# A mixed attention and expert kernel whose attention orders and PSUM banks are taken from a list planner

## The chip, the cores and the metric

The kernel runs on one core of one Trainium2 chip. The metric is the device time of the whole launch in microseconds (us). The core's engines, as the profile names them, are PE (TensorE, matmuls; PEld is its loading of weights), ACT (ScalarE), DVE (VectorE), POOL (GpSimd) and SP (SyncE, which here only issues DMAs). Each works through its own queue in order, and a step waits on semaphores for steps of other engines.

## What is computed

The reference is a cross-attention with 16 heads of 32 and then a mixture of 8 experts, in which every expert takes its best 512 of the 4096 tokens. Cut to what matters:

```python
x = x + attention(layernorm(x), ctx)     # x, ctx: 8 x 512 x 512
#   q = h @ Wq + bq, k = ctx @ Wk + bk, v = ctx @ Wv + bv
#   softmax(q k^T / sqrt(32)) v, then @ Wo + bo
xf = layernorm(x).reshape(4096, 512)
prob = softmax(xf @ Ws + bs).T           # 8 experts
vals, routes = top_k(prob, 512)
h = gelu(xf[routes] @ W1 + b1)           # 512 x 2048, per expert
out = (h @ W2 + b2) * vals               # added to x at routes
```

## The kernel before

Attention runs in 32 groups: 8 batches of 512 tokens, and in each of them 4 groups of 4 heads (r is the group's number within its batch, 0 to 3). Products with weights keep 32-bit accuracy by splitting each operand in a high and a low part and adding three matmuls, so a projection of a group is 12 matmuls of 512 columns for K and 12 for Q, the values 48 a batch, the output projection 48 a batch.

A group g passes through these steps, named as in the code:

- proj (K and Q, two groups ahead): PE, then the high part on ACT, the low part on DVE (proj_lo); SP writes both to memory (keep_hi, keep_lo) and reads them back in a stacked form (stack_hi, stack_lo) into kst and qst, of which there are three each.
- max (one group ahead), 16 tiles: PE multiplies (L1730), DVE takes each row's extreme (L1339), ACT computes the exponentials in place for the sums (sum, L1143). The tile's bank is returned only then. Then rows: PE transposes the maxima (L1747), ACT and DVE split them (L1134, L1347), and POOL copies them by two small DMAs into qst (rows_lo, L1037). The scores of the group wait for these rows.
- score, 16 tiles: PE (L1762), exponential on ACT into one of six buffers p_ring (L1155); att: for every four of them PE multiplies with the values into the single bank ps_att (L1773). After the fourth att of a group comes divide on DVE (L1371), then osplit and osplit_lo.
- per batch: loading and splitting of the context and of x (csplit, stats, norm, turn), the values v (L1685), the two halves of the output projection (outa, out), the second norm (x1_norm), and the router (route, logits, back).

Seven of the eight PSUM banks (ps_gen) are shared by all steps but att. A class Agenda holds one list of steps. attention_agenda walks through the groups in 20 slots each, with the 16 scores and the 4 att steps at fixed slots, and puts every other step at a hand-set place in units of a group: MAX_AT = ((-0.11, 0.59), ...) by r, ROWS_AT = 0.70, END_MAX_AT for the last group's maxima, and so on. The list in order of these places is the order of TensorE's queue. Each other engine takes the same list, shifted by hand-set lags by kind (order_of). Banks go round: take_bank gives the bank that was given longest ago and is not kept open by a projection:

```python
    def take_bank(self, key):
        i = next(k for k in self.bank_order if k not in self.bank_open)
        self.bank_order.remove(i)
        self.bank_order.append(i)
```

The steps before group 0 (first loads, weights, the first projections and maxima) are listed by hand. After attention come the choice of tokens by bisection, and the experts.

## Time and profile before

| | |
|---|---|
| median of 3 runs | 1729.57 us (1729.15 to 1729.82) |
| span of the profiled execution, first to last instruction | 1729.0 us |
| mean granted TensorE clock, as a share of 2.4 GHz | 0.973 |
| PE, DVE, ACT, POOL busy | 1620.6, 1110.7, 983.9, 303.9 us |
| DMA traffic | 217.27 MB, mean 126 GB/s |

The profiled execution is one run, and its span is 0.6 us below the median of the runs. Starts in the rows are microseconds from the span's start. A row of instructions gives start, duration, engine, line of the kernel, operation, tile written and tiles read, and in square brackets how long the engine had been idle before and what ended the wait. Matmuls overlap: the next one starts before the last one ends, so the distance of the starts is what one costs.

### The profile page before, as it was taken

What the parts mean: (1) busy time and instruction counts of PE and PEld (TensorE: products, weight loads), DVE (VectorE), ACT (ScalarE), POOL (GpSimd) and SP (SyncE); (2) the same over time, 40 slices, a digit from 0 to 9 for tenths busy, and PEclk for the clock granted to TensorE, in tenths of its full rate; (3) what the DMA queues carried; (4) which work ended last, traced back from release to release, by engine and by line L of the source; (5) the groups of instructions that cost most, each with busy time, mean ns of one, the idle gap of its engine ahead of it and who ended that gap; (6) DMA issues with size and microseconds to landing.
All of it is one profiled execution on the core that took longest, in us unless ns stands there. A gap on an engine that the chain in (4) does not pass through costs nothing.

```text
span 1729.0 us, 22299 instructions
## 1 busy us (share of the span) xinstructions
PE 1620.6 (94%) x7847; PEld 1163.4 (67%) x7847; DVE 1110.7 (64%) x1950; ACT 983.9 (57%) x2115; POOL 303.9 (18%) x396
## 2 busy tenths in 40 slices
PE   7889899899898998999987699999999999999997
PEld 5546566566565664655644488788888888888885
DVE  7576876867768678587664566766454545454543
ACT  5798897987988979888875222223232323232321
POOL 5121221311303112113012010102020202020110
PEclk9999899999999999999989899999999999999999
DMA  5452744635436436263351132435243433334340
GB/s 180 122 170 68 214 120 126 176 96 169 138 92 197 141 123 182 65 205 122 111 183 63 43 123 98 120 107 152 98 139 111 114 131 96 136 99 151 97 123 25
DMA packets 131271, 217.27 MB, mean 126 GB/s; under 512 B 17116, under 2 KB 51056, under 8 KB 131160
## 3 DMA queue, kind: packets, MB, share of 16 engines
q1 hardware_dynamic: 114520, 173.23, 32.3%
q0 software_dynamic: 16640, 42.61, 8.9%
q8 instruction: 63, 1.03, 0.3%
q14 instruction: 48, 0.39, 0.1%
HBM read 157.45 MB, written 57.82 MB: 125 GB/s over the span
## 4 chain that ended last, share of the span: by engine, by line
PE 79%; DVE 9%; ACT 6%; issue 3%; DMA 2%; SPq 0%; POOL 0%; DVEq 0%; POOLq 0%
PE ps_gen L751 8%; PE ps_gen L753 8%; PE ps_gen L752 8%; PE ps_gen L1926 7%; PE ps_gen L1928 7%; PE ps_gen L1927 7%; PE ps_att L1773 6%; PE ps_gen L1730 5%; PE ps_gen L1762 5%; PE ps_gen L1712 3%; ACT ps_gen L1143 3%; PE ps_gen L1713 3%; PE ps_gen L1714 3%; ACT p_ring L1155 2%; DVE stat L1243 2%
## 5 line engine op out<-in xcount | busy, mean ns | idle before, releaser
L1339 DVE TENSOR_REDUCE nmax<-ps_gen 128x1 f32<-128x512 f32 x512 | 338.3, 684 | 128.4 <-PE ps_gen L1730 127.7
L1143 ACT ACTIVATE ps_gen<-ps_gen,nmax 128x512 f32<-128x512 f32 x512 | 343.2, 675 | 57.7 <-DVE nmax L1339 57.7
L1155 ACT ACTIVATE p_ring<-ps_gen,keep_scale 128x512 f32<-128x512 f32 x512 | 336.5, 695 | 61.9 <-PE ps_gen L1762 61.9
L1212 ACT ACTIVATE gel<-ps_gen,b_cols 128x512 f32<-128x512 f32 x128 | 88.3, 690 | 448.8 <-PE ps_gen L753 448.7
L1594 DVE TENSOR_TENSOR gel_lo<-gel,gel_hi 128x512 fp32r<-128x512 f32 x126 | 87.2, 692 | 281.6 <-ACT gel_hi L1213 277.3
L1730 PE MATMUL ps_gen<-kst,qst 97*128 97x512 f32 x512 | 208.2, 429 | 16.8 <-ACT ps_gen L1143 11.2
L1762 PE MATMUL ps_gen<-qst,kst 99*128 99x512 f32 x512 | 195.3, 432 | 16.0 <-ACT ps_gen L1143 11.8
L751 PE MATMUL ps_gen<-hT_hi,w_hi 128*128 128x512 f32 x512 | 202.2, 395 | 0.2 <-DVE hT_lo L1587 0.2
L753 PE MATMUL ps_gen<-hT_hi,w_lo 128*128 128x512 f32 x512 | 199.5, 390 | 0.0
L752 PE MATMUL ps_gen<-hT_lo,w_hi 128*128 128x512 f32 x512 | 199.4, 389 | 0.0
L1926 PE MATMUL ps_gen<-w_hi,gel_hi 128*128 128x512 f32 x504 | 198.1, 393 | 0.0
L1928 PE MATMUL ps_gen<-w_hi,gel_lo 128*128 128x512 f32 x504 | 196.5, 390 | 0.0
L1927 PE MATMUL ps_gen<-w_lo,gel_hi 128*128 128x512 f32 x504 | 196.3, 389 | 0.0
L1773 PE MATMUL ps_att<-p_ring,v_sb 128*32 128x512 f32 x1024 | 147.5, 650 | 4.1 <-ACT p_ring L1155 4.0
L1762 PEld LDWEIGHTS ps_gen<-qst,kst 99*128 99x128 f32 x512 | 95.3, 197 | 79.9 <-issue 30.4
L1730 PEld LDWEIGHTS ps_gen<-kst,qst 97*128 97x128 f32 x512 | 98.4, 195 | 63.1 <-ACT ps_gen L1143 24.2
L1065 POOL DMA_INDIRECT out_x<-y_out,idx x28 | 49.5, 1768 | 511.1 <-ACT y_out L1232 504.7
L1143 ACT ACTIVATION_READ_ACCUMULATOR ps_gen<-ps_gen,nmax 128x1 f32 x512 | 113.4, 221 | 0.0
L753 PEld LDWEIGHTS ps_gen<-hT_hi,w_lo 128*128 128x128 f32 x512 | 96.1, 188 | 20.6
L751 PEld LDWEIGHTS ps_gen<-hT_hi,w_hi 128*128 128x128 f32 x512 | 96.2, 188 | 19.5 <-issue 0.6
L752 PEld LDWEIGHTS ps_gen<-hT_lo,w_hi 128*128 128x128 f32 x512 | 96.2, 188 | 19.3
L1928 PEld LDWEIGHTS ps_gen<-w_hi,gel_lo 128*128 128x128 f32 x504 | 94.6, 188 | 19.9
(218 smaller groups left out, 2687.4 us busy)
## 6 DMA issues: line engine op xcount, KB each, us to landing
w_raw<-in_L_ffn_W SPq DMA_DIRECT2D x128, 512.0 KB, 3.5
kst<-qk_rows SPq DMA_DIRECT2D x93, 256.0 KB, 3.9
qst<-qk_rows SPq DMA_DIRECT2D x93, 256.0 KB, 5.1
x_in<-in_x POOLq DMA_DIRECT2D x60, 256.0 KB, 3.4
out_x<-x_in SPq DMA_DIRECT2D x32, 256.0 KB, 2.6
qk_rows<-kT_hi SPq DMA_DIRECT2D x31, 256.0 KB, 2.0
qk_rows<-kT_lo SPq DMA_DIRECT2D x31, 256.0 KB, 2.0
qk_rows<-qT_hi SPq DMA_DIRECT2D x31, 256.0 KB, 2.0
```

Of the source, the lines that this page charges most:

```text
L751: e.matmul(psum, lhsT=wh, rhs=mh, start=(i == 0), stop=False)
L752: e.matmul(psum, lhsT=wh, rhs=ml, start=False, stop=False)
L753: last = e.matmul(psum, lhsT=wl, rhs=mh, start=False, stop=(i == n - 1))
L1143: e.activation(psum[:, :], psum[:, :], ACT.Exp, bias=nmax[g % 2][:, c], scale=-1.0, accum_out=den[g % 2][:, c]).then_inc(drained_sem("max" ...
L1155: e.activation(p_ring[n % NP_][:, :], ps("score", g, kt, h)[:, :], ACT.Exp, scale=keep_scale[:, b:b + 1]).then_inc(drained_sem("score", g, ...
L1339: e.tensor_reduce(nmax[g % 2][:, h * TB + t:h * TB + t + 1], ps("max", g, h, t)[:, :], AX.X, ALU.min).then_inc(s_min, 1)
L1730: e.matmul(ps("max", g, h, t)[:, :], lhsT=qst[k][0:ROWS_MAX, h, t * P:(t + 1) * P], rhs=kst[k][0:ROWS_MAX, h, :], start=True, stop=True).t ...
L1762: e.matmul(ps("score", g, kt, h)[:, :], lhsT=kst[k][0:ROWS_ALL, h, kt * P:(kt + 1) * P], rhs=qst[k][0:ROWS_ALL, h, :], start=True, stop=Tr ...
L1773: last = e.matmul(ps_att[h * DH:(h + 1) * DH, :], lhsT=v_sb[:, kt, (c4 * HG + h) * DH:(c4 * HG + h + 1) * DH], rhs=p_ring[((g * KT + kt) * ...
L1926: e.matmul(ps_y[tt], lhsT=gh, rhs=wh, start=(j == 0), stop=False)
L1927: e.matmul(ps_y[tt], lhsT=gh, rhs=wl, start=False, stop=False)
L1928: return e.matmul(ps_y[tt], lhsT=gl, rhs=wh, start=False, stop=(j == NF - 1))
```

## The change

The single list goes. Every step becomes a Part on an engine, with the parts that it comes after, a wanted time, the bank that it takes or gives back, and two costs from a table (how long the engine is occupied, and when the result is seen). Parts of one kind on one engine form a line and keep their order among themselves. Plan.run then goes forward in modelled time: of the parts at the heads of the lines it takes those that can start within LOOK of the earliest, and of these the one with the smallest wanted time. That gives every engine its own order. A part that takes a bank gets the one that is expected back first; HELD limits max tiles to three banks and scores to two. The wanted times are again places in units of a group (K_AT, Q_AT, MAX_AT, SPAN) plus LAG by engine and kind. The steps before group 0 keep their order. The closing steps of a batch's router become steps of their own (choice_max, choice_exp, choice), the special places of the last group's maxima go, and the hand-written end of attention is planned too. The instructions themselves and what each waits for stay as they are. The K projection of the group two after an r=3 group is wanted at -0.698 to -0.096 of it instead of 0.05 to 0.10.

```diff
+class Part:
+
+    def __init__(self, engine, step, at, cost, after, line, takes, frees):
+        self.engine, self.step, self.at = engine, step, at
+        self.busy, self.seen = cost
+        self.after, self.line = after, line
+        self.takes, self.frees = takes, frees
+        self.ready = None
...
+    def add(self, engine, step, at, after=(), line=None, takes=None, frees=None):
+        line = (engine, line or step[0])
+        part = Part(engine, step, at + LAG.get(line, 0), COST[engine][step[0]], after, line, takes, frees)
+        self.parts[(engine,) + step] = part
+        self.lines.setdefault(line, []).append(part)
+
+    def run(self):
+        a = self.agenda
+        for line in self.lines.values():
+            line.sort(key=lambda part: part.at)
+        head = {line: 0 for line in self.lines}
+        lines_of = {engine: [line for line in self.lines if line[0] == engine] for engine in a.order}
+        free = {engine: 0.0 for engine in a.order}
+        bank_free = {i: 1e-3 * n for n, i in enumerate(a.bank_order)}
+        held = {}
+        returned = {kind: [] for kind in HELD}
+        taken = {kind: 0 for kind in HELD}
+
+        def startable(part):
+            start = 0.0
+            for need in part.after:
+                before = self.parts.get(need)
+                if before is None:
+                    continue
+                if before.ready is None:
+                    return None
+                start = max(start, before.ready)
+            if part.takes:
+                if not bank_free:
+                    return None
+                start = max(start, min(bank_free.values()) + 0.05)
+                kind = part.takes[0]
+                if kind in HELD:
+                    n = taken[kind] - HELD[kind]
+                    if n >= len(returned[kind]):
+                        return None
+                    if n >= 0:
+                        start = max(start, sorted(returned[kind])[n])
+            if part.engine == "pe" and start > 0:
+                start += 0.107
+            return max(start, free[part.engine])
+
+        left = len(self.parts)
+        while left:
+            best = None
+            for engine in a.order:
+                able = []
+                for line in lines_of[engine]:
+                    if head[line] < len(self.lines[line]):
+                        part = self.lines[line][head[line]]
+                        start = startable(part)
+                        if start is not None:
+                            able.append((start, part))
+                if able:
+                    first = min(start for start, _ in able)
+                    start, part = min((p for p in able if p[0] <= first + LOOK), key=lambda p: (p[1].at, p[0]))
+                    if best is None or start < best[0]:
+                        best = (start, part)
+            start, part = best
+            left -= 1
+            head[part.line] += 1
+            free[part.engine] = start + part.busy
+            part.start, part.ready = start, start + part.seen
+            a.order[part.engine].append(part.step)
+            if part.takes:
+                i = min(bank_free, key=bank_free.get)
+                del bank_free[i]
+                held[part.takes] = i
+                a.give_bank(part.takes, i)
+                if part.takes[0] in HELD:
+                    taken[part.takes[0]] += 1
+            if part.frees:
+                bank_free[held[part.frees]] = part.ready
+                if part.frees[0] in HELD:
+                    returned[part.frees[0]].append(part.ready)
...
-
-    GAPS = 5 * KT
-    K_AT = ((0.01, 0.35), (-0.13, 0.22), (0.05, 0.15), (0.05, 0.10))
-    Q_AT = ((0.40, 0.42), (0.21, 0.30), (0.14, 0.34), (0.17, 0.32))
-    MAX_AT = ((-0.11, 0.59), (-0.07, 0.66), (-0.05, 0.67), (-0.17, 0.60))
-    ROWS_AT = 0.70
-    RECIP_AT, RDEN_AT, OSPLIT_AT = 0.03, 0.56, 0.18
-    V_NEXT_AT = (0.32, 1.32)
-    LOAD_C_AT, SPLIT_C_AT = (-0.26, 0.33), (0.29, 0.48)
-    LOAD_X_AT, STATS_X_AT = (0.28, 0.41), (0.66, 0.95)
-    NORM_X_AT, TURN_X_AT = (0.71, 1.05), (0.93, 1.16)
-    HALF_AT, HALF_FOR = (("residual", 0.03), ("add_bias", 0.35), ("outa", 0.49)), 0.76
-    LATE_AT = (("out", 0.20), ("x1_norm", 0.44), ("route", 0.56), ("logits", 0.66), ("back", 0.73))
-    LATE_FOR = 0.74
...
-    END_MAX_AT, END_ROWS_AT = (-0.39, 0.56), 0.68
...
+ENGINES = ("pe", "act", "dve", "pool", "sync")
+COST = {
+    "pe": {"proj": (0.693, 0.89), "max": (0.231, 0.43), "rows": (0.109, 0.31), "rden": (0.436, 0.63), "score": (0.231, 0.43),
+           "att": (1.105, 1.15), "v": (2.74, 2.94), "turn": (0.436, 0.63), "outa": (1.386, 1.59), "osum": (0.693, 0.89),
+           "out": (1.386, 1.59), "route": (0.436, 0.63), "logits": (0.405, 0.52), "back": (0.109, 0.31)},
+    "act": {"proj": (0.585, 0.73), "sum": (0.662, 0.82), "rows": (0.174, 0.30), "score": (0.570, 0.72), "osplit": (0.613, 0.79),
+            "csplit": (0.520, 0.66), "turn": (0.477, 0.64), "logits": (0.157, 0.31), "route": (0.477, 0.64),
+            "choice_exp": (0.136, 0.26), "wsplit": (0.585, 0.72)},
+    "dve": {"proj_lo": (0.658, 0.78), "max": (0.600, 0.72), "rows_lo": (0.313, 0.32), "recip": (0.160, 0.30), "rden": (0.597, 0.72),
+            "divide": (0.592, 0.72), "osplit_lo": (0.659, 0.78), "v": (0.570, 0.72), "csplit_lo": (0.600, 0.72),
+            "stats": (1.020, 1.10), "norm": (0.453, 0.57), "turn_lo": (0.598, 0.72), "outa": (0.600, 0.72), "out": (1.750, 1.80),
+            "x1_norm": (0.453, 0.57), "route": (0.602, 0.72), "back": (0.300, 0.35), "choice_max": (0.330, 0.41),
+            "choice": (0.540, 0.60), "wsplit": (0.660, 0.78), "tables": (0.500, 0.60)},
+    "pool": {"rows_lo": (1.050, 2.60), "recip": (0.560, 0.66), "load": (0.550, 4.00), "load_wo": (0.550, 3.30),
+             "residual": (0.550, 4.00), "stats": (0.600, 0.75), "add_bias": (1.240, 1.39), "out": (0.600, 0.75),
+             "tables": (12.0, 12.0)},
+    "sync": {"keep_hi": (0.360, 2.30), "keep_lo": (0.360, 2.30), "stack_hi": (0.800, 6.00), "stack_lo": (0.400, 5.50),
+             "mask_row": (0.400, 2.50), "out": (0.360, 3.00), "x1_norm": (0.360, 3.00), "choice_out": (0.360, 2.50),
+             "piece_in": (0.800, 3.00)},
+}
+LOOK = 0.023
+HELD = {"max": 3, "score": 2}
+LAG = {
+    ("act", "proj"): 0.065, ("dve", "proj_lo"): 0.032, ("pool", "rows_lo"): -0.605, ("act", "rows"): -0.136, ("dve", "rows_lo"): -0.141,
+    ("sync", "stack_hi"): -0.046, ("sync", "stack_lo"): 0.395, ("pool", "recip"): 0.043, ("dve", "rden"): -0.186, ("dve", "outa"): -0.4,
+    ("dve", "csplit_lo"): -0.274, ("dve", "turn_lo"): 0.082, ("dve", "v"): 0.188, ("dve", "out"): 0.019, ("act", "turn"): 0.006,
+    ("dve", "back"): -0.047, ("act", "osplit"): -0.275, ("dve", "divide"): 0.345, ("act", "logits"): -0.091, ("pool", "add_bias"): -0.545,
+    ("act", "csplit"): -0.079, ("pe", "rows"): 0.166, ("dve", "route"): -0.071, ("dve", "max"): -0.081, ("dve", "recip"): -0.034,
+    ("act", "score"): 0.027, ("act", "sum"): 0.034, ("pe", "score"): -0.219, ("dve", "osplit_lo"): 0.15,
+}
+K_AT = ((0.24, 0.248), (-0.055, 0.281), (0.094, 0.256), (-0.698, -0.096))
+Q_AT = ((0.472, 0.472), (0.34, 0.351), (0.109, 0.318), (0.248, 0.412))
+MAX_AT = ((0.124, 0.67), (0.036, 0.694), (-0.083, 0.753), (0.309, 0.742))
+ROWS_AT, RECIP_AT, RDEN_AT, OSPLIT_AT, ATT_AT = 0.132, 0.197, 0.833, -0.55, 0.042
+SPAN = {
+    "v": (-1, 0.295, 1.594), "load_c": (-3, -0.536, 0.13), "csplit": (-3, -0.167, -0.092), "load_x": (-3, 0.752, 0.887),
+    "stats": (-3, 0.587, 0.597), "norm": (-3, 0.577, 0.856), "turn": (-3, 0.676, 0.826), "residual": (2, -0.159, 0.515),
+    "add_bias": (2, 1.445, 2.219), "outa": (2, 0.138, 0.992), "out": (4, 0.006, 0.738), "x1_norm": (4, 0.603, 1.647),
+    "route": (4, 0.389, 1.208), "logits": (4, 0.608, 1.2), "back": (4, 0.751, 1.343),
+}
+
+
+def spread(span, k, n):
+    return span[0] + (span[1] - span[0]) * (k + 0.5) / n
...
+                p.add("pe", ("max", g, h, t), at, stacks if n == 0 else [], takes=("max", g, h, t))
+                p.add("dve", ("max", g, h, t), at, [("pe", "max", g, h, t), ("pe", "rows", g - 2), ("act", "sum", g - 2, HG - 1, TB - 1)])
+                p.add("act", ("sum", g, h, t), at, [("dve", "max", g, h, t), ("dve", "recip", g - 2)], frees=("max", g, h, t))
...
+            for h in range(HG):
+                n = (g * KT + kt) * HG + h
+                at = g + (kt + h / HG) / KT
+                p.add("pe", ("score", g, kt, h), at, [("pool", "rows_lo", g)], takes=("score", g, kt, h))
+                p.add("act", ("score", g, kt, h), at,
+                      [("pe", "score", g, kt, h), ("pe", "att", *divmod((n - NP_) // HG, KT))], frees=("score", g, kt, h))
+            p.add("pe", ("att", g, kt), g + (kt + 1) / KT + ATT_AT,
+                  [("act", "score", g, kt, HG - 1), ("dve", "v", b, kt), ("dve", "divide", g - 1)])
+        p.add("dve", ("divide", g), g + 1, [("pe", "att", g, KT - 1), ("dve", "rden", g)])
+        used = [("pe", "outa" if r < GB // 2 else "out", b - 1, TB - 1)]
...
-            for kind, *at in steps:
+            for kind, *at in agenda.order["pe"]:
```

## Rows read from the trace of the kernel before

**Rows 1.** The page: span, busy time by engine, chain that ended last, one group of instructions.

```profile
span 1729.0 us, 22299 instructions
...
PE 1620.6 (94%) x7847; PEld 1163.4 (67%) x7847; DVE 1110.7 (64%) x1950; ACT 983.9 (57%) x2115; POOL 303.9 (18%) x396
...
PE 79%; DVE 9%; ACT 6%; issue 3%; DMA 2%; SPq 0%; POOL 0%; DVEq 0%; POOLq 0%
...
L1155 ACT ACTIVATE p_ring<-ps_gen,keep_scale 128x512 f32<-128x512 f32 x512 | 336.5, 695 | 61.9 <-PE ps_gen L1762 61.9
```

**Rows 2.** Stretches: start:end, length, busy us of PE PEld DVE ACT POOL, PEclk, DMA share, GB/s.

```profile
534.00:646.00 112.00, 104.37 (x534) 66.62 (x532) 82.78 (x161) 94.51 (x221) 22.94 (x35) 0.98 0.48 142
...
992.00:1729.00 737.00, 724.52 (x3393) 595.05 (x3391) 407.04 (x571) 200.52 (x318) 89.14 (x64) 0.99 0.37 113
...
81.00:937.00 856.00, 796.89 (x3980) 500.61 (x3980) 615.68 (x1178) 719.47 (x1660) 174.88 (x277) 0.96 0.46 138
```

**Rows 3.** Stretches of one batch, cut where divide (L1371) starts; columns as in rows 2.

```profile
533.50:560.50 27.00, 22.59 (x121) 12.43 (x120) 23.86 (x55) 24.10 (x57) 7.42 (x13) 0.94 0.61 168
560.50:587.10 26.60, 24.42 (x121) 15.24 (x120) 19.65 (x34) 25.52 (x62) 7.56 (x11) 1.00 0.46 139
587.10:615.00 27.90, 27.90 (x137) 19.15 (x136) 15.66 (x27) 22.29 (x51) 2.50 (x4) 1.00 0.35 95
615.00:646.40 31.40, 30.36 (x164) 20.46 (x163) 24.51 (x51) 23.36 (x54) 5.83 (x10) 1.00 0.51 160
```

**Rows 4.** Groups of PE instructions, 81 to 937 us: count, busy us, mean ns, idle before.

```profile
L1730 PE MATMUL ps_gen<-kst,qst 97*128 97x512 f32 x477 | 195.8, 429 | 14.9 <-ACT ps_gen L1143 11.0 <-issue 3.7
L1762 PE MATMUL ps_gen<-qst,kst 99*128 99x512 f32 x494 | 188.0, 431 | 15.4 <-ACT ps_gen L1143 11.3 <-DVE qT_lo L1324 1.8 <-DMA qst<-by_row 1.8
...
L751 PE MATMUL ps_gen<-wv_hi,cT_hi 128*128 128x512 f32 x112 | 43.9, 392 | 0.0
```

**Rows 5.** Timeline of PE, 498 to 513 us.

```profile
499.93 1.06 PE L1773 MATMUL ps_att<-p_ring,v_sb 128*32 128x512 f32 x8
...
505.88 0.39 PE L752 MATMUL ps_gen<-wv_lo,cT_hi 128*128 128x512 f32 x1
506.11 0.39 PE L753 MATMUL ps_gen<-wv_hi,cT_lo 128*128 128x512 f32 x1
```

**Rows 6.** Waits of PE, 81 to 937 us: us in total, times, longest us.

```profile
PE ps_gen L1747 <- DVE nmax L1339: 15.7, 14, 1.4
PE ps_gen L1762 <- ACT ps_gen L1143: 11.3, 17, 1.0
PE ps_gen L1730 <- ACT ps_gen L1143: 11.0, 10, 1.3
```

**Rows 7.** Chain that ended last, 450 to 570 us: start, us, engine, tile, line.

```profile
461.63 0.44 PE ps_gen L1754 x4
...
523.40 0.71 DVE stat L1243
...
525.37 0.53 POOL qst L1037
525.90 3.99 DMA qst<-by_row
```

**Rows 8.** Timeline of PE, 515 to 566 us.

```profile
546.80 0.91 PE L1730 MATMUL ps_gen<-kst,qst 97*128 97x512 f32 x2 [1.21 <-ACT ps_gen L1143]
547.65 1.94 PE L1773 MATMUL ps_att<-p_ring,v_sb 128*32 128x512 f32 x8
```

**Rows 9.** Timelines of PE and SP around 887 us.

```profile
889.12 0.40 PE L1730 MATMUL ps_gen<-kst,qst 97*128 97x512 f32 x1
893.19 0.77 PE L1730 MATMUL ps_gen<-kst,qst 97*128 97x512 f32 x1 [3.67 <-issue]
...
887.11 0.30 SPq L853 DMA_DIRECT2D qst<-qk_rows  x1
```

**Rows 10.** DMA issues, 81 to 937 us: count, KB each, median us to landing.

```profile
qst<-by_row POOLq DMA_DIRECT2D x60, 8.0 KB, 1.7
```

More of the change, by code:

```diff
@@ L67, in __init__ @@
         self.steps = []
-        self.times = []
-        self.now = -3.0
+        self.order = {}
         self.bank = {}
@@ L87, in add @@
     def add(self, *step):
-        if self.now < 0 or self.now >= NG:
-            self.now += 1e-4
         self.steps.append(step)
-        self.times.append(self.now)
-    def order_of(self, lags):
-        def at(n):
-            inside = 0 <= self.times[n] < NG
-            return self.times[n] + (lags.get(self.steps[n][0], 0) if inside else 0)
-        return [self.steps[n] for n in sorted(range(len(self.steps)), key=at)]
     def flush(self):
@@ L324, in attention_agenda @@
-    END_MAX_AT, END_ROWS_AT = (-0.39, 0.56), 0.68
-    places = []
-    def place(start, span, calls):
-        lo, hi = start + span[0], start + span[1]
-        for k, call in enumerate(calls):
-            places.append((lo + (hi - lo) * (k + 0.5) / len(calls), call))
-    def late(kind, b, t):
-        if kind == "residual":
-            a.residual(b, t)
-        elif kind == "out":
-            a.out(b, t)
-        elif kind in ("outa", "route", "logits", "back"):
-            a.with_bank(kind, b, t)
-        else:
-            a.add(kind, b, t)
@@ L371, in attention_agenda @@
-    place(NG - 2, (0.0, 0.1), [(a.add, "piece_in", n) for n in range(3)])
-    place(NG - 2, (0.1, 0.2), [(a.add, "tables")])
-    place(0, (0.0, 0.3), [(a.load_wo, c) for c in range(DC)])
-    place(0, (0.4, 0.85), [(a.add, "wsplit", "o", c) for c in range(DC)])
-    places.sort(key=lambda p: p[0])
-    def fill(time):
-        a.now = time - 1 / GAPS
-        a.flush()
-        while places and places[0][0] < time:
-            call, *args = places.pop(0)[1]
-            call(*args)
-    def attend(g, kt):
-        a.add("att", g, kt)
-        if kt == KT - 1:
-            a.add("divide", g)
@@ L389, in attention_agenda @@
-    for i in range(NG):
-        for kt in range(KT):
-            before = (i, kt - 1) if kt else (i - 1, KT - 1)
-            time = [i + (5 * kt + n) / GAPS for n in range(1, 6)]
-            a.now = i + kt / KT
-            a.with_bank("score", i, kt, 0)
-            a.with_bank("score", i, kt, 1)
-            fill(time[0])
-            if before[0] >= 0:
-                attend(*before)
-            fill(time[1])
-            a.with_bank("score", i, kt, 2)
-            fill(time[2])
-            a.with_bank("score", i, kt, 3)
-            fill(time[3])
-            fill(time[4])
-        a.flush()
@@ L406, in attention_agenda @@
-    a.now = NG + 1.0
-    attend(NG - 1, KT - 1)
-    for t in range(TB):
-        a.osum(B - 1, t)
-    a.osplit(NG - 1)
-    a.flush()
-    for t in range(TB):
-        a.out(B - 1, t)
-        if t > 0:
-            a.add("x1_norm", B - 1, t - 1)
-    a.add("x1_norm", B - 1, TB - 1)
-    for t in range(TB):
-        a.with_bank("route", B - 1, t)
-    for kind in ("logits", "back"):
-        for t in range(TB):
-            a.with_bank(kind, B - 1, t)
+    a.order = {engine: list(a.steps) for engine in ENGINES}
@@ L774, in load_b2 @@
                 e.dma_start(b2_b[k][:, :], b2[ex:ex + 1, :].to_broadcast([P, D])).then_inc(s_b2[k], 16)
[L776 removed]
+            for kind, *at in agenda.order["sync"]:
                 if kind == "first":
@@ L919, in gpsimd_program @@
             e.memset(half[:, :], -0.5).then_inc(s_const, 1)
-            for kind, *at in agenda.order_of(agenda.lags["pool"]):
+            for kind, *at in agenda.order["pool"]:
                 if kind == "picks":
@@ L1083, in scalar_program @@
             on = Waiter(e)
-            for kind, *at in agenda.order_of(agenda.lags["act"]):
+            for kind, *at in agenda.order["act"]:
                 if kind == "turn":
```

274 lines of the change are left out of this document (174 added, 100 removed).

## The prediction, made before the changed kernel was run

> **What bounds the kernel now.** I read the page first. TensorE is busy 94% of the 1729.0 us span, and the chain that ended last is 79% TensorE, 9% VectorE, 6% ScalarE [rows 1]. That mean hides two halves, so I cut the span with the view by stretches [rows 2]. From 992 us on, in the experts, TensorE is busy 724.5 of 737.0 us at clock 0.99; the change does not touch that code. Attention, 81 to 937 us, is another case: 796.9 of 856 us, granted clock 0.96, ScalarE 719.5, VectorE 615.7. "Busy" flatters TensorE here, since a matmul's 0.39 us overlaps the next one's start, 0.23 us later [rows 5].
>
> So I counted the work of a batch (four groups). By the code it has 64 max, 64 score, 96 projection, 48 value and 48 output matmuls of 512 columns. The trace's counts agree: 477 max and 494 score matmuls in the 31 groups of the stretch, 112 for each third of the value product of 7 batches [rows 4]. 320 x 0.23 = 73.6 us. The 16 attention-value steps (eight matmul records each, x8) take 1.06 us each at full clock [rows 5], 17.0 us; at half clock one takes 1.94 us [rows 8]. Twelve groups of four transposes at 0.44 us [rows 7] are 5.3, and logits, single transposes and the like I estimate at 2. Sum: 98 us of TensorE at full clock, against 112 to 114 us that a batch takes. About 14 us a batch, 12%, are lost.
>
> Where? I cut one batch at the starts of the VectorE divide that ends each group (the one from 533.5 to 646.4 us) [rows 3]. First stretch (early r=1): 27.0 us, TensorE 22.6, ScalarE 24.1, VectorE 23.9, clock 0.94. Second (r=2): 26.6 us, ScalarE 25.5. Third (r=3): 27.9 us, TensorE all of it, ScalarE only 22.3. Fourth (r=0 of the next batch): 31.4 us, TensorE 30.4, ScalarE 23.4. So the limits alternate: the exponentials limit two groups, matmuls (values, output projection) the other two, and only the difference between the columns is a stall.
>
> The view of waits names TensorE's own stalls in attention: 15.7 us in 14 pieces where the transpose of the maxima stood at the head of TensorE's queue for the last reduction, 11.3 and 11.0 us where a score or a max matmul waited for ScalarE to give its bank back [rows 6]. Two single places stand out in the timeline. A burst of output tiles on VectorE (the statistics at 523.40) makes the max rows late, and their DMA, issued 525.37, is 3.99 us of the chain [rows 7]. At 889.1 to 893.2 us TensorE stands for a max matmul of the last group, whose operand left SyncE only at 887.11; after it the same matmul shows 0.77 us, half clock [rows 9].
>
> **The change, part by part.** *Instructions.* None is added or removed in attention: same matmuls, exponentials, reductions and DMAs with the same waits. The step that closed a batch's router is split in two, so that VectorE can do something between subtracting the maximum and summing, 0.3 us at most, seven times: 2 us on VectorE, which is not the limit. I take nothing. The experts do not change: 0.
>
> *Banks.* Before, a bank was chosen by rotation in TensorE's order, whichever was free. Now it is the one the plan expects back first, with at most 3 held by max tiles and 2 by scores, leaving 2 for projections and the rest. That aims at the 11.3 + 11.0 us of bank waits. Floor nothing, ceiling 22.3. A score holds a bank for a matmul (0.43 us at L1762's mean [rows 4]) plus an exponential (0.695 [rows 1]): about 1.2 us with the signals between, two banks give one score each 0.6 us, near ScalarE's own pace, so I take the limit of 2 to cost nothing while sums run between scores.
>
> *Order on TensorE.* The transpose of the maxima is no longer placed at a fixed 0.70 of the group; it is queued when the plan sees the last reduction done. That aims at the 15.7 us [rows 6]. But where ScalarE is the limit, removed TensorE idling is only partly time.
>
> *Order on ScalarE and VectorE.* Hand lags become a choice of the earliest startable step. This is what can close the gaps in the first and second stretches. If they ran at ScalarE's busy time, and the other two at TensorE's, a batch would take 24.1 + 25.5 + 27.9 + 30.4 = 107.9 us instead of 112.9: 5.0 us. That is the most that ordering alone gives; more needs matmuls moved from the long stretches into the short ones. The tables do some of that: the K projection wanted in group r=3 goes 0.7 of a group earlier (4 x 3 x 0.23 = 2.8 us), turns and output halves about 0.3 earlier. But these land in r=2, where TensorE already has 24.4 of 26.6 us, so I count no gain for it. The whole batch cannot go under the 98 us of matmul.
>
> I take half of the 5.0 us, 2.5 a batch, over 7 batches: 17.5 us. Half, because ScalarE's busy column overlaps the reading of its accumulator with the next exponential and so overstates what it must do, while each chain matmul, reduction, exponential has latencies that no order removes. The ends are 0 and 35 (7 x 5.0).
>
> *The last groups.* The hand-set place of the last group's maxima, -0.39 of a group, is what put them in front of the queue before their DMA was there [rows 9]. The plan gives these loads 5.5 to 6.0 us and schedules other work first. TensorE idled 3.67 us there and then ran cold; but scores would have waited on the same maxima later. I take 3 of it (0 to 6). After 937 us the output tiles are a VectorE chain that a new order of transposes shortens by 1 us at most; I take 0.
>
> *What the plan gets wrong.* It fixes each queue for durations that never vary. The max rows cost 2.6 us from issue in it. The trace has 0.5 us for issuing and a median of 1.7 to landing [rows 10] for each of two, which agrees, but also 0.53 + 3.99 = 4.5 us in a busy stretch [rows 7], 1.9 more. Scores are pulled 0.219 of a group ahead, so a late row finds TensorE's head blocked. In one boundary of five of the 31: 6 x 0.4 to 1.9 us, I take 3 (0 to 59).
>
> Sum against the profiled 1729.0: - 17.5 - 3 + 3 = -17.5 us, 1711.5. The runs' median of 1729.57 is 0.6 above the span, so 1712; I say **1711**.
>
> The clock. TensorE's granted clock drops to 1.2 GHz about once a batch: two max matmuls at 546.80 after 1.21 us of idling, and then an x8 step taking 1.94 us instead of 1.06 [rows 8]. Fewer pauses should leave fewer of these; at one drop a batch it is worth 1 to 2 us a batch and is inside my 2.5.
> The Trainium skill (TensorE: Matmul & The Clock Gate, section "A second HAM failure mode: psum-queue depth-cycling") speaks against a planner like this one: frequent short pauses between groups of matmuls while cycling through banks can make the clock oscillate. The trace agrees so far only at one place a batch.
>
> **The rivals.**
> *A. The stretches are already at their limits.* For: TensorE is busy 27.9 of 27.9 us in one stretch and 30.4 of 31.4 in another, ScalarE 25.5 of 26.6 in a third [rows 3]; only the first has room. Then I gain 1 us a batch or less and the waits only change names: 1729.6 - 5 = 1724, from 1720 to 1732.
> *B. The plan levels the batch.* TensorE and ScalarE are limits in different groups, and the order now lets ready matmuls fill any gap. If a batch came to 106, that is 7 us each, 49, and 5 at the ends: 1676, from 1665 to 1692. Against: value tiles can't leave PSUM before the batch's last attention steps have read the old ones, and 2 banks remain for them.
> *C. Late rows block the queue (slower).* The mechanism is that of the last part: TensorE reaches the next group's first score when the plan expects the rows, and max matmuls, projections and attention-value steps stand behind it. The gain of 20.5 is used up, and 3.5 more lost, at 24 / 31 = 0.8 us a boundary. With 1.2 us in each, 1729.6 - 20.5 + 37 = 1746. Against: the median landing of 1.7 us fits the plan [rows 10].
> *D. The pauses get shorter and more, and the clock oscillates.* If a further 10 us of each batch ran at 1.2 GHz, with TensorE the limit, that is 5 us x 7 = 35: 1712 + 35 = 1747. The rule cited above is this one. For: one drop a batch already follows a pause of 1.2 us. Against: the clock is 1.00 in three stretches of four [rows 3], though they have many pauses below 1 us.
>
> **How the numbers follow.** My forecast, 1696 to 1720, 0.42; B 0.20; A 0.20; C 0.13; D 0.05. A measurement of this kernel tells about 0.2%, 3.5 us, from no change. Faster: 0.42 + 0.20 + half of A, 0.10, is 0.72. Same: the rest of A, 0.09. Slower: C, D and a trace of A, 0.19. The range leaves out the lower half of B (0.08) and the upper halves of C and D (0.10): 1678 to 1743. Both signs in it; the forecast's own range is 1696 to 1720.
>
> **What would show it.** Right: the divides stand 110 to 111 us apart over a batch instead of 113; TensorE's wait for nmax at the transpose of maxima under 5 us in all (15.7 before); the two bank waits halved; no 3.7 us stop near 890. The first stretch of a batch shrinks most, the third stays at 27.9. Wrong, C: TensorE's score matmuls wait for DMA qst<-by_row for tens of us. Wrong, B: ScalarE over 24.5 us in the stretch that has 22.3 now. Wrong, D: granted clock under 0.93 over attention. Wrong in another way: the busy engine of a stretch is not its limit, the loop through three engines and seven banks is; then the gain would not stand in the first stretch but in all four.

## The result, and the profile after

The changed kernel takes 1691.61 us (median of 4 runs, 1688.73 to 1693.09) against 1729.69 us: 38.1 us less, a ratio of 0.9774 with a 95% interval of 0.976 to 0.9788. The forecast was 1711, with a range of 1678 to 1743. The sign and the range hold; the gain is twice the 18 us that I had worked out. The profiled execution is the one of 1688.73 us, the fastest of the four, with a span of 1686.9; so the two spans differ by 42.1 us, the medians by 38.1.

The page of the changed kernel, the same lines as in [rows 1]:

```profile
span 1686.9 us, 22363 instructions
...
PE 1601.5 (95%) x7847; PEld 1164.9 (69%) x7847; DVE 1113.7 (66%) x1950; ACT 978.3 (58%) x2115; POOL 301.6 (18%) x396
...
PE 82%; DVE 7%; DMA 4%; ACT 4%; issue 2%; POOL 0%; SPq 0%; DVEq 0%; POOLq 0%; ACTq 0%
```

The number of matmuls is the same (x7847). In the chain TensorE has gained three points, ScalarE and VectorE have lost two each, and DMA has doubled, from 2% to 4%. Attention as a whole, which answers to the last line of [rows 2], and a batch cut at the starts of divide, which answers to [rows 3]:

```profile
77.00:893.80 816.80, 779.60 (x3987) 501.71 (x3985) 619.41 (x1178) 715.57 (x1663) 170.56 (x274) 0.98 0.48 144
```

```profile
501.10:531.40 30.30, 29.15 (x158) 18.75 (x159) 28.79 (x63) 29.19 (x69) 11.57 (x19) 1.00 0.65 196
531.40:553.90 22.50, 22.50 (x112) 14.68 (x113) 15.85 (x27) 21.46 (x53) 4.60 (x6) 1.00 0.50 139
553.90:578.70 24.80, 24.80 (x122) 16.53 (x123) 15.74 (x27) 22.48 (x54) 1.16 (x3) 1.00 0.26 74
578.70:605.60 26.90, 26.86 (x156) 17.87 (x156) 23.63 (x49) 21.29 (x50) 5.68 (x10) 1.00 0.61 191
```

Read this beside [rows 3]. The batch takes 104.5 us in place of 112.9. Three of its four stretches are now TensorE from end to end, and the clock is 1.00 in all. TensorE idles 1.2 us in the whole batch; before it was 7.6. The first stretch, the only one in which I had seen room, became longer, 30.3 us for 27.0, and took in 158 TensorE instructions in place of 121. Every other stretch is shorter by 3 to 4.5 us. Work has moved into the first stretch. What moved, the view by stretches says when asked for one line alone: the first of the three matmuls of each K or Q projection step, here the kernel before (its line L1712),

```profile
533.50:560.50 27.00, 2.71 (x7) 1.13 (x6) 0.94 0.61 168
560.50:587.10 26.60, 3.57 (x8) 1.50 (x8) 1.00 0.46 139
587.10:615.00 27.90, 3.42 (x9) 1.50 (x8) 1.00 0.35 95
615.00:646.40 31.40, 3.84 (x10) 1.89 (x10) 1.00 0.51 160
```

and here the changed kernel (L1853):

```profile
501.10:531.40 30.30, 6.08 (x15) 2.83 (x15) 1.00 0.65 196
531.40:553.90 22.50, 2.87 (x7) 1.32 (x7) 1.00 0.50 139
553.90:578.70 24.80, 2.05 (x5) 0.94 (x5) 1.00 0.26 74
578.70:605.60 26.90, 2.07 (x5) 0.94 (x5) 1.00 0.61 191
```

7, 8, 9, 10 have become 15, 7, 5, 5. (A batch has 32 such steps; the rows of before add up to 34, because a matmul that runs across a cut is counted on both sides. The weight loads, the second count, give 6, 8, 8, 10.) Eight more steps of three matmuls at 0.23 us are 5.5 us of TensorE, moved into the stretch where it idled. By the kind of matmul it is the next batch's K projections that moved, from 3 to 11 steps in that stretch; Q stays at 4. The other 13 of the 37 added instructions are three max and three score matmuls and seven transposes of x. In the plan's own list for TensorE, the K projections of the next batch's first two groups come after 1.56 and 1.81 groups' worth of scores; before they came after 2.12 and 3.12 (counted from the start of the batch under way).

The waits of TensorE in attention, which answer to [rows 6]:

```profile
PE ps_gen L1903 <- DMA qst<-by_row: 9.5, 7, 2.9
PE ps_gen L1871 <- DMA qst<-qk_rows: 7.8, 1, 7.8
PE ps_gen L1871 <- DVE qT_lo L1459: 5.5, 6, 0.9
...
PE ps_gen L1871 <- ACT ps_gen L1278: 3.0, 11, 0.8
...
PE ps_gen L1888 <- DVE nmax L1474: 0.8, 1, 0.8
```

The wait of the maxima's transpose is down from 15.7 us to 0.8, the two waits for ScalarE to give a bank back from 22.3 to 3.2. By the code a max matmul that waits for qT_lo waits for a bank too, one that a projection held; that is 5.5 us now. The scores' wait for late rows (L1903) is up to 9.5 us from 1.8. One wait is new: a single 7.8 us.

Where did the 42.1 us between the two spans go? By the starts of divide: to the first one +1.9 (80.9, 82.7); from there over 28 groups to the divide at 873.3 before, 821.3 after, -53.9; over the last three groups, 63.6 before and 72.5 after, +8.9; behind the last divide +1.0. So the full batches gain 7.7 us each, and the end gives 9 back. The 28 groups as one stretch, before and after:

```profile
80.90:873.30 792.40, 742.90 (x3732) 473.47 (x3733) 582.78 (x1116) 667.36 (x1544) 161.71 (x248) 0.97 0.47 140
```

```profile
82.70:821.30 738.60, 718.35 (x3707) 469.58 (x3707) 580.29 (x1106) 656.98 (x1533) 160.06 (x249) 0.99 0.50 149
```

The 53.9 us have three parts. TensorE idles 20.2 us in place of 49.5: 29.3 us. It has 25 matmuls fewer here, since about that many more now run before the first divide (279 for 253): at 0.23 us about 6 us. The rest is mostly the clock: cut into pieces of 2 us, the granted clock adds up to 44 us at 1.2 GHz before and 10 us after. At that level matmuls of 512 columns start 0.43 us apart (those at 409.92 to 411.20, for instance) in place of 0.23, so 34 us less of it are worth up to 16. These three make 51 of the 53.9 us; the clock's part is up to 30% of them.

What happened at the end, the queue of SyncE shows, in the changed kernel from 829 us:

```profile
832.69 0.40 SPq L900 DMA_DIRECT2D w_raw<-in_L_ffn_W  x1
833.13 0.50 SPq L902 DMA_DIRECT2D w_raw<-in_L_ffn_W  x1
...
834.72 1.39 SPq L946 DMA_DIRECT2D qk_rows<-qT_hi  x1
836.14 0.49 SPq L900 DMA_DIRECT2D w_raw<-in_L_ffn_W  x1
836.67 0.86 SPq L902 DMA_DIRECT2D w_raw<-in_L_ffn_W  x1
837.63 0.48 SPq L953 DMA_DIRECT2D qk_rows<-qT_lo  x1
838.15 0.53 SPq L900 DMA_DIRECT2D w_raw<-in_L_ffn_W  x1
838.72 1.55 SPq L902 DMA_DIRECT2D w_raw<-in_L_ffn_W  x1
842.97 0.81 SPq L977 DMA_DIRECT2D qst<-qk_rows  x2
```

and the chain that ended last, and TensorE:

```profile
834.72 8.24 DMA qk_rows<-qT_hi
843.35 8.50 DMA qst<-qk_rows
```

```profile
852.74 1.62 PE L1871 MATMUL ps_gen<-kst,qst 97*128 97x512 f32 x3 [7.77 <-DMA qst<-qk_rows]
```

Of six weight loads of 512 KB, two go out just before the write of the last group's Q and four between that write and the read back: the plan sees SyncE's queue free and knows no bandwidth. The write takes 8.24 us, the stacked read 8.50, and TensorE stands for 7.77.

### The profile page after: what moved, and what is told of

The parts are those of the page before. It is cut to its first block, busy times and chain, and to the rows that moved or that the text cites. A ratio compares the mean times of both kernels' runs of the same rounds, so it can differ in the third digit from the quotient of the medians.

```text
span 1686.9 us, 22363 instructions
## 1 busy us (share of the span) xinstructions
PE 1601.5 (95%) x7847; PEld 1164.9 (69%) x7847; DVE 1113.7 (66%) x1950; ACT 978.3 (58%) x2115; POOL 301.6 (18%) x396
## 4 chain that ended last, share of the span: by engine, by line
PE 82%; DVE 7%; DMA 4%; ACT 4%; issue 2%; POOL 0%; SPq 0%; DVEq 0%; POOLq 0%; ACTq 0%
PE ps_gen L886 9%; PE ps_gen L887 8%; PE ps_gen L888 8%; PE ps_gen L2067 7%; PE ps_gen L2069 7%; PE ps_gen L2068 7%; PE ps_gen L1903 7%; PE ps_gen L1871 6%; PE ps_att L1914 6%; PE ps_gen L1853 3%; PE ps_gen L1854 3%; PE ps_gen L1855 3%; ACT ps_gen L1278 2%; PE ps_gen L1930 2%; PE ps_gen L1931 2%
## 5 line engine op out<-in xcount | busy, mean ns | idle before, releaser
L1474 DVE TENSOR_REDUCE nmax<-ps_gen 128x1 f32<-128x512 f32 x512 | 330.0, 683 | 78.6 <-PE ps_gen L1871 76.7
L1903 PE MATMUL ps_gen<-qst,kst 99*128 99x512 f32 x512 | 196.8, 425 | 10.7 <-DMA qst<-by_row 9.5
L1871 PE MATMUL ps_gen<-kst,qst 97*128 97x512 f32 x512 | 186.6, 423 | 17.9 <-DMA qst<-qk_rows 7.8
L1903 PEld LDWEIGHTS ps_gen<-qst,kst 99*128 99x128 f32 x512 | 95.3, 190 | 96.6 <-issue 66.0
L1871 PEld LDWEIGHTS ps_gen<-kst,qst 97*128 97x128 f32 x512 | 93.8, 191 | 79.8 <-issue 40.1
L1914 PE MATMUL ps_att<-p_ring,v_sb 128*32 128x512 f32 x1024 | 139.5, 617 | 5.4 <-ACT p_ring L1290 5.2
L1200 POOL DMA_INDIRECT out_x<-y_out,idx x28 | 49.5, 1770 | 511.1 <-ACT y_out L1367 504.7
```

The costliest lines, as they stand in the source:

```text
L1474: e.tensor_reduce(nmax[g % 2][:, h * TB + t:h * TB + t + 1], ps("max", g, h, t)[:, :], AX.X, ALU.min).then_inc(s_min, 1)
L1871: e.matmul(ps("max", g, h, t)[:, :], lhsT=qst[k][0:ROWS_MAX, h, t * P:(t + 1) * P], rhs=kst[k][0:ROWS_MAX, h, :], start=True, stop=True).t ...
L1903: e.matmul(ps("score", g, kt, h)[:, :], lhsT=kst[k][0:ROWS_ALL, h, kt * P:(kt + 1) * P], rhs=qst[k][0:ROWS_ALL, h, :], start=True, stop=Tr ...
L1914: last = e.matmul(ps_att[h * DH:(h + 1) * DH, :], lhsT=v_sb[:, kt, (c4 * HG + h) * DH:(c4 * HG + h + 1) * DH], rhs=p_ring[((g * KT + kt) * ...
```

## The experiments

Times are medians with the ratio to the kernel before, run beside them on the same chip (its medians were 1728.52 to 1730.34 us), and the ratio's 95% interval.

**Banks alone.** The kernel before, all orders kept; its lists are run through the plan as one line for each engine.

```diff
+    for engine, kept in head.items():
+        lags = old.lags.get(engine, {})
+        steps = old.steps if engine == "pe" else old.order_of(lags)
...
+                    part.line, part.at = (engine, "all"), at
...
-HELD = {"max": 3, "score": 2}
+HELD = {}
```

> The kernel before with all five engines' orders unchanged, step by step; only the PSUM banks are given out as the plan gives them (the one expected back first), without limits on the banks held. Theory O (the gain of 38 us comes from the orders, which keep TensorE filled in three of four stretches): little, -5 to +3 us against before. Theory K (banks: the waits of 11.3 + 11.0 us for a bank were the price of the rotation): -10 to -20 us, and both waits below 5 us.

1727.72 us, 0.999 (0.9979 to 1.0). Nothing that can be told from no change, as Theory O expected. The waits of max and score matmuls (L2254, L2286) for an exponential of the maxima (L1661) to return a bank fell from 22.3 to 5.8 us, each of the two below the 5 us that Theory K named, but the time did not follow. Waits for an exponential of the scores (L1673), which return banks as well, came in their place, and the transpose's wait for the last reduction rose to 18.1:

```profile
PE ps_gen L2271 <- DVE nmax L1857: 18.1, 14, 1.6
...
PE ps_gen L2286 <- ACT p_ring L1673: 4.2, 7, 0.6
PE ps_gen L2254 <- ACT ps_gen L1661: 4.1, 14, 0.7
...
PE ps_gen L2254 <- ACT p_ring L1673: 2.3, 7, 0.8
PE ps_gen L2286 <- ACT ps_gen L1661: 1.7, 10, 0.2
```

So the waits for ScalarE to return a bank fell by 10 us, from 22.3 to 12.3, and were worth under 2 us of time: where TensorE had waited for a bank, it now waits a little later for something else.

**Orders alone.** The planned orders, step by step, but a turn among the banks:

```diff
+    for part in p.done:
+        if part.takes:
+            i = next(k for k in turn if k in back)
...
+        if part.frees:
+            back.add(holder[part.frees])
```

> The changed kernel with the planned orders unchanged; each step that takes a bank takes the one that was taken longest ago among those whose return stands before it in the plan, in place of the one expected back first. Theory O: 1690 to 1698 us, nearly all of the gain kept. Theory K: 1705 us or more, with TensorE's waits on ScalarE for banks back above 15 us in all.

1748.93 us, 1.0109 (1.0086 to 1.0132): 57 us behind the changed kernel, with the same orders. Theory O falls in this form. The time is Theory K's, its sign is not: TensorE's waits on ScalarE for a bank stay under 7 us in all. TensorE now waits where it did not before, for banks that projections and values hold:

```profile
PE ps_gen L1887 <- DVE qT_lo L1475: 15.9, 20, 1.6
PE ps_gen L1887 <- DVE v_sb L1529: 8.9, 20, 0.5
...
PE ps_gen L1887 <- DVE kT_lo L1475: 5.4, 6, 0.9
```

The turn is counted by the plan's sequence of steps, so a bank can be taken that comes back later than another; the turn of the kernel before itself was not run, since by the lists steps would then wait for each other in a circle. What the run says is that these orders need the banks they were made with.

**Planner with the places of before.** New Plan.run and limits, old wanted times and lags.

```diff
-K_AT = ((0.24, 0.248), (-0.055, 0.281), (0.094, 0.256), (-0.698, -0.096))
+K_AT = ((0.01, 0.35), (-0.13, 0.22), (0.05, 0.15), (0.05, 0.10))
...
-    "v": (-1, 0.295, 1.594), "load_c": (-3, -0.536, 0.13), "csplit": (-3, -0.167, -0.092), "load_x": (-3, 0.752, 0.887),
+    "v": (-1, 0.32, 1.32), "load_c": (-3, -0.26, 0.33), "csplit": (-3, 0.29, 0.48), "load_x": (-3, 0.28, 0.41),
```

> The changed kernel's planner and its limits on the banks, but with the wanted times and the lags by kind that the kernel before has. Theory O1 (the procedure, ready steps first on each engine, makes the gain): 1690 to 1703 us. Theory O2 (the wanted times do, the planner is only their carrier): 1710 to 1735 us, with stretches again at 27, 27, 28 and 31 us.

1766.79 us, 1.0203 (1.0168 to 1.0237). The planner as a procedure is 37 us slower than the hand-set lists if it is fed with their numbers, and slower than either theory allowed. TensorE stands 18.5 us for the second norm (its output, transposed for the router) and 19.9 us, up to 4.2 us at a time, for a max matmul.

**No lags.** `LAG = {}`.

> The changed kernel without the table of lags by engine and kind (all zero); wanted times by group as changed. Theory O1: within 8 us of the changed kernel's 1691.6. Theory O2: 1705 us or more, since the score lag of -0.219 and the late divide and stacks are what orders the engines.

1689.87 us, 0.9774 (0.9757 to 0.979). All 29 lags together are worth nothing that shows. It serves as the base of the next runs, since it is simpler.

**The places in two halves,** both on top of no lags.

```diff
-MAX_AT = ((0.124, 0.67), (0.036, 0.694), (-0.083, 0.753), (0.309, 0.742))
-ROWS_AT, RECIP_AT, RDEN_AT, OSPLIT_AT, ATT_AT = 0.132, 0.197, 0.833, -0.55, 0.042
+MAX_AT = ((-0.11, 0.59), (-0.07, 0.66), (-0.05, 0.67), (-0.17, 0.60))
+ROWS_AT, RECIP_AT, RDEN_AT, OSPLIT_AT, ATT_AT = 0.70, 0.03, 0.56, 0.18, 0.05
```

(and K_AT and Q_AT) for the first; the whole of SPAN for the second.

> The changed kernel without lags, and with the places of before for the steps of a group (K, Q, maxima, rows, reciprocal, denominators, output split); the steps of a batch keep the changed places. Theory G (the group's places carry the gain, by what they let TensorE do early): 1720 us or more. Theory S (the batch's places carry it): below 1705 us.

1705.14 us, 0.9854 (0.9828 to 0.988): 15 us more than its base, a hair outside what Theory S named. So much hangs on the group's places.

> The changed kernel without lags, and with the places of before for the steps of a batch (loads, splits, statistics, turns, values, output halves, router); the group's places as changed. Theory G: below 1705 us. Theory S: 1720 us or more, since TensorE then stands for norms at the turns.

1757.57 us, 1.0148 (1.0111 to 1.0186): 68 us, more than the whole gain, hang on the batch's places: Theory S by the time. Not by its reason, since TensorE does not stand for norms; its longest wait is 15.0 us in all in front of a max matmul.

**No limits on the banks held.** `HELD = {}` in the changed kernel.

> The changed kernel without the limits of 3 banks for max tiles and 2 for scores. If the limits carry the gain: 1710 us or more, because maxima, wanted early, fill the banks and projections find none. If they are only a bound that the order hardly meets: within 5 us of 1691.6.

1799.0 us, 1.0395 (1.0366 to 1.0424), 107 us behind. And with the limit of 3 for max tiles kept, `HELD = {"max": 3}`:

> The changed kernel with only the limit of 3 banks for max tiles, scores unlimited. If the 107 us of e7 are maxima that hold banks for two engines' work: within 8 us of 1691.6. If they are scores run ahead of the exponentials: 1750 us or more.

1759.08 us, 1.0153 (1.0127 to 1.018). So the limit of two for scores is worth 67 us, that for maxima another 40 once the scores have none. Without the score limit the wait of score matmuls for the maxima's rows is the longest, in both runs; here in the run with the limit for maxima alone:

```profile
PE ps_gen L1903 <- DMA qst<-by_row: 31.5, 18, 3.0
```

That is 22 us more than in the changed kernel, a third of the 67. That scores run ahead of the exponentials, as the expectation has it, fits the time; no run shows it apart.

**The pieces of the experts after the last stacked loads.**

```diff
+    landed = [("sync", "stack_" + k, w, NG - 1) for k in ("hi", "lo") for w in "kq"]
     for n in range(3):
-        p.add("sync", ("piece_in", n), NG - 2, done)
+        p.add("sync", ("piece_in", n), NG - 2, landed)
```

> The changed kernel, but the loads of the first three expert pieces come after the four stacked loads of the last group in the plan, in place of between them. If the 3 MB of weights are what makes those loads take 8.2 and 8.5 us in the chain (and the stretch from 821 to 856 us 35 us long): 1680 to 1686 us. If the stretch is long for another reason: 1691 us and no change.

1682.59 us, 0.9731 (0.9702 to 0.976), 9.0 us less than the changed kernel and inside what was expected. The weights go out behind the stacked loads:

```profile
843.29 0.79 SPq L978 DMA_DIRECT2D qst<-qk_rows  x2
...
844.60 0.50 SPq L989 DMA_DIRECT2D qst<-qk_rows  x1
845.20 0.40 SPq L901 DMA_DIRECT2D w_raw<-in_L_ffn_W  x1
```

The last three groups take 62.5 us here, 72.5 in the changed kernel and 63.6 before, and the 7.8 us stop is gone. The same write of Q takes 4.7 us in place of 8.24, and the stacked reads a median of 3.5 in place of 8.50. So the 9 us that the end had given back are these 512 KB loads. (The profiled spans differ by 5.5 us only. In this execution the 28 groups took 3.3 us more, at nearly the same idle time of TensorE, with 24 us at the lower clock in place of 10.)

**Preparing the next batch, and the output side,** each with the places of before, on top of no lags. First loads, split, statistics, norms and turns, then all the rest of SPAN.

> The changed kernel without lags (e4, 1689.9 us), with the places of before for the steps that prepare the next batch alone: loads, split of the context, statistics, norms, turns. Theory P (the 67 us of e6 come from preparing late: projections of the next batch stand for the turned x and the split context): 1725 us or more. Theory Q (they come from the output side): within 8 us of e4.

1757.13 us, 1.0134 (1.0103 to 1.0166): all of e6's loss, so Theory P by the time. TensorE's longest waits are those in front of a max matmul (14.7 us), for exponentials (14.3) and for late rows (13.4), not the projections' own.

> The same, with the places of before for values, residual, bias, output halves, second norm and router alone. Theory P: within 8 us of e4. Theory Q: 1725 us or more.

1714.0 us, 0.9887 (0.9861 to 0.9913): 24 us, between the two expectations. The halves do not add up, 67 and 24 are more than 68; both theories named something.

Then the preparation was split: the context, and x.

```diff
-    "v": (-1, 0.295, 1.594), "load_c": (-3, -0.536, 0.13), "csplit": (-3, -0.167, -0.092), "load_x": (-3, 0.752, 0.887),
+    "v": (-1, 0.295, 1.594), "load_c": (-3, -0.26, 0.33), "csplit": (-3, 0.29, 0.48), "load_x": (-3, 0.752, 0.887),
```

is the first of the two; the second takes load_x, stats, norm and turn back instead.

> The changed kernel without lags (1689.9 us), with the places of before for the loads and the split of the context alone. If the K projections of the next batch, which need the split context, are what must come early: 1715 us or more, and the projection count in the first stretch near 7 again in place of 15. If the turns must: within 8 us of 1689.9.

1735.25 us, 1.003 (1.0013 to 1.0046), 45 us behind its base. The longest stretch of a batch (32.9 us) has 10 projection steps, neither the 15 of the changed kernel nor the 7 of before.

> The same with the places of before for the loads of x, statistics, norms and turns alone. If the context carries it: within 8 us of 1689.9. If the turns must come early: 1715 us or more.

1727.85 us, 0.9996 (0.9975 to 1.0016), 38 us behind. Here the long stretch has 14 projection steps, as good as the changed kernel, and yet takes 33.7 us where that one takes 30.3. The chain in it shows why:

```profile
535.29 5.53 DMA qk_rows<-kT_hi
541.77 3.99 DMA qk_rows<-qT_hi
546.13 3.85 DMA qst<-qk_rows
549.98 2.13 issue
```

A projection that comes late goes to memory and back before its max matmuls can run, and TensorE stood 3.67 us for the first of them. (The profile names no releaser for the last 2.13 us; the read of the low part, issued only at 547.26, may be it.) Such stops add up to 24.5 us in seven places. So preparing early does two things: it gives TensorE matmuls for the stretch where it had none, and it covers the round trip through memory.

**Late rows in the plan.** On top of e8, the plan is told what a busy stretch had shown: `"rows_lo": (1.050, 4.50)` in place of 2.60.

> The kernel of e8 (1682.6 us), with the plan's duration for the maxima's rows raised from 2.60 to 4.50 us, what a busy stretch showed. If late rows at the head of TensorE's queue cost what the waits name (9.6 us): 1675 to 1681 us. If what is put ahead of them instead is no better: 1680 to 1690 us.

1702.32 us, 0.9822 (0.9795 to 0.985), 20 us slower than e8, outside both expectations. The wait for the rows left the list of the longest, and a worse one came:

```profile
PE ps_gen L1854 <- DVE cT_lo L1411: 26.5, 6, 5.7
```

A K projection of the next batch stood at TensorE's head for the split of the context, 5.7 us at the worst. Why this plan puts it there I can't say; a more truthful number made a worse list.

**The moved matmuls in the hand-set list.** The kernel before with

```diff
-    K_AT = ((0.01, 0.35), (-0.13, 0.22), (0.05, 0.15), (0.05, 0.10))
+    K_AT = ((0.01, 0.35), (-0.13, 0.22), (-0.40, -0.20), (-0.698, -0.096))
```

> The kernel before, unplanned, with two of its hand-set places changed: the K projection two groups ahead is placed at -0.40 to -0.20 of an r=2 group and -0.698 to -0.096 of an r=3 group (before 0.05 to 0.15 and 0.05 to 0.10). These are the matmuls that the plan moves into the stretch where TensorE had room. If moving them is all that the planner does: 1700 to 1715 us. If one list for all engines cannot carry it (the stacked loads of the early projection stand in SyncE's queue for scores not yet made, in front of the next Q's): 1728 us or more.

1768.73 us, 1.0226 (1.0209 to 1.0244), 39 us slower than before:

```profile
PE ps_gen L1762 <- ACT ps_gen L1143: 19.0, 25, 1.0
PE ps_gen L1712 <- DVE xT_lo L1269: 15.9, 7, 2.5
PE ps_gen L1730 <- ACT ps_gen L1143: 13.1, 15, 1.2
```

The bank waits grew from 22.3 to 32.1 us and the Q projection's wait for the turned x from 4.8 to 15.9. The first matmuls of the projection steps in the first two stretches of the batch from 555.7 us:

```profile
555.70:583.50 27.80, 3.83 (x10) 1.71 (x9) 1.00 0.71 202
583.50:618.70 35.20, 4.21 (x8) 1.89 (x8) 0.85 0.33 101
```

Three steps moved into the first stretch, not eight: I had taken the wanted time of the second of the two K projections, and in this list that puts it at 2.44 to 2.88 groups' worth of scores, where the plan's own list has it at 1.81 to 2.06. So the run shows that these places are bad in this list, 8.6 us worse in r=2 alone; it does not carry the plan's move over, and whether the hand-set list could have carried that, with context and x prepared earlier as well, was not run. That SyncE's queue blocks, as I had guessed, these lines neither show nor exclude.

**Both simplifications.** No lags, pieces late.

> The changed kernel without lags and with the expert pieces loaded after the last stacked loads. If the two do not touch each other: 1689.9 - 9.0 = 1681 us, 1677 to 1685, no faster than e8 (1682.6).

1680.54 us, 0.9715 (0.9697 to 0.9732), the best of the study, 11 us below the changed kernel; the difference to e8 is inside the runs' spread.

## Why the prediction was wrong in size, and right in sign

*What bounds the kernel* held. The 98 us of TensorE work in a batch are a floor, a batch now takes 104.5 us and more, and the alternation of limits that I read from [rows 3] was there, and was what could be gained.

*The step that failed* is this sentence: "But these land in r=2, where TensorE already has 24.4 of 26.6 us, so I count no gain for it." With it I capped the gain at 5.0 us a batch, "the most that ordering alone gives", and took half. The batches gained 7.7 us each. The matmuls landed in the first stretch, not in r=2: I had taken the wanted time for the place. In a planner it is only a priority, and a step that is ready goes earlier. The context is wanted earlier in the same change, and so are the statistics, norms and turns of x (its loads later); e9, e14 and e15 show that both, the context and x, carry 67, 45 and 38 us. (They show it for this planner, whose numbers were set together; early preparation alone in the old list was not run.) The signs of being right that I had named say the same: the first stretch, which was to shrink most, grew, and the third, which was to stay at 27.9 us, fell to 24.8. This is my rival B, levelling, with its 106 us a batch (104.5 in the batch shown; by the starts of divide, the first batch took 100.0, the other six 104.5 to 110.4); I gave it 0.20 because I thought the values would hold it back. B is not right in all: its 5 us of gain at the ends were a loss, and its sign, ScalarE over 24.5 us in the third stretch, did not come (22.5); ScalarE's work grew in the first stretch, from 24.1 to 29.2. The values stayed where they were (12 and 4 of their first matmuls in the third and fourth stretch, in both kernels); projections moved instead.

*Half of 5.0 us a batch*: forecast -17.5, measured -53.9 over the 28 groups, of which 29.3 are less idling, about 6 work done before them and up to 16 the clock.

*Banks.* I took the limit of two for scores to cost nothing, and put the bank part at 0 to 22.3 us of gain. What I missed is that without limits the planner is a loss of 70 us on the kernel before (e7). The banks' choice alone is nothing in the old order (e1) and 57 us in the new one (e2). Less of a named wait was no measure of time.

*Order on TensorE.* The transpose's wait fell from 15.7 to 0.8 us, as forecast under 5.

*The last groups.* Forecast -3, measured +8.9. The 3.67 us stop of [rows 9] did go, and a 7.77 us stop of the same matmul came, from six DMAs whose move I had not followed: I counted no DMA of piece_in, though the plan lets SyncE send it as soon as the projections end. In the kernel before, the first of them left at 887.99 us, after the last stacked load (887.11). e8 settles it: with the pieces late the last three groups are 1 us shorter than before, so my 3 was too much even then.

*What the plan gets wrong, and rival C.* Late rows at TensorE's head cost 9.5 us of waits in place of 1.8, nearer to my 3 than to C's 37. That a cure exists by telling the plan the longer time is refuted by e12, for this one value.

*The clock* is the second term that I had too small: "worth 1 to 2 us a batch and is inside my 2.5". I had read it from the one fall of one batch. Over seven batches TensorE stood at 1.2 GHz for 44 us, 6.3 a batch, and the 0.96 over attention in [rows 2] could have told me. With 10 us left, the clock gave back up to 2.3 us a batch, nearly as much as my whole forecast for one. That it did so because the pauses became fewer is how the traces read (TensorE's idling fell from 49.5 to 20.2 us, and in e13 both rose, to 68 us idle and 72 us at 1.2 GHz); no run holds one of the two still.

*Rival D* did not come: the granted clock over attention rose from 0.96 to 0.98, and it is 1.00 in all four stretches of the batch shown. It is low around the 7.77 us stop, 0.64 over these 19 us. But it fell before the stop, which begins near 845 us, after pauses of 0.78 and 1.20 us:

```profile
834.00:853.00 19.00, 8.59 (x30) 3.08 (x31) 6.20 (x14) 10.24 (x26) 3.32 (x12) 0.64 0.90 267
```

```profile
839.50:844.50 5.00, 3.42 (x12) 1.03 (x12) 0.77 (x3) 3.48 (x9) 1.63 (x3) 0.50 1.07 359
```

The rule of the Trainium skill on cycling through banks (TensorE: Matmul & The Clock Gate, section "A second HAM failure mode: psum-queue depth-cycling") is not tested by this kernel: its condition is many short pauses, and here the pauses got fewer.

*Rival A* fell: the stretches were at their limits, but the limits could be moved against each other.

## What to carry to other kernels

When the busy columns of two engines alternate from stretch to stretch, add up each engine over the whole period before you take the stretch as fixed: the larger sum, not the sum of the larger ones, is the floor, and what it takes to approach it is to have the inputs of movable work ready early. In a list planner, wanted times are priorities and so say little about where a step lands; its limits on shared buffers may be worth more than its whole gain, and its numbers are tuned together, so that one made truer can cost 20 us. Read the granted clock as a loss of its own, over the whole period and not from one place: each microsecond at the lower level costs up to half of itself. Follow every DMA whose release the plan moves, since a planner that knows queues but no bandwidth will send megabytes in front of a load that everything waits for.

## What the runs showed of the hardware

A 256 KB write to memory (qk_rows<-qT_hi) has a median of 2.0 us to landing over attention. Among six 512 KB loads, two sent before it and four behind, the same write took 8.24 us and the stacked read after it 8.50 us, at a DMA share of 0.90 and 267 GB/s in the stretch; with the loads behind both (e8) the write took 4.7 us and the stacked reads 3.5.

TensorE's granted clock fell to 1.2 GHz in each of the seven batches of the kernel before, after pauses of 0.9 to 1.4 us (1.21 us in front of the max matmuls at 546.80, for one), and stood there for 44 us in all; in the changed kernel it was 10 us. And a change that takes 10 us of bank waits off TensorE (e1) moved the time by 0.1%.
